# A gated cross-attention and mixture-of-experts block on one core: batches 2 and 3 prepared ahead of slot 0, the first values placed over two queues with the weight loads held behind them, K and V of chunk 2 in slot 0

## The reference

```python
def _L0_xattn_ref(x, y, Wq, bq, Wkv, bkv, Wo, bo):      # h = 16 heads, dh = 8
    q = (jnp.einsum('bld,ed->ble', x, Wq) + bq).reshape(b, l, h, dh)
    kv = (jnp.einsum('bmc,ec->bme', y, Wkv) + bkv).reshape(b, m, h, 2 * dh)
    k, v = (kv[..., :dh], kv[..., dh:])
    att = jax.nn.softmax(jnp.einsum('blhd,bmhd->blmh', q, k) * scale, axis=2)
    out = jnp.einsum('blmh,bmhd->blhd', att, v).reshape(b, l, d)
    return jnp.einsum('bld,ed->ble', out, Wo) + bo

def _more_forward(x, Wg, bg, W1, b1, W2, b2):           # E = 4 experts, top 2, R = 4 rounds
    cur = x
    for r in range(R):
        logits = flat @ Wg[r] + bg[r]
        ...                                             # softmax over the two best, weights cw
        hmid = jax.nn.gelu(jnp.einsum('nh,ehf->enf', flat, W1) + b1[:, None, :])
        y = jnp.einsum('enf,efh->enh', hmid, W2) + b2[:, None, :]
        cur = cur + jnp.einsum('ne,enh->nh', cw, y).reshape(b, s, h)
    return cur

x = x + jnp.tanh(g_xattn[0]) * _L0_xattn_ref(_layernorm(x), ctx_768, ...)
x = x + jnp.tanh(g_ffn[0]) * _L0_ffn_ref(_layernorm(x), ...)
```

## Time and profile before

| what | value |
|---|---|
| median of 3 runs | 466.93 us |
| the profiled execution | 467.07 us, of which the span of the engines is 465.3 us |
| PE busy | 451.0 us, 97% of the span |
| ACT, DVE, POOL busy | 370.3, 361.6, 69.6 us |
| attention stage | to 92.1 us, where the first expert matmuls start |
| fourth issue of SP, x of batches 2 and 3 | at 2.17 us |

### The profile page before, as it was taken

The page is one execution under the profiler, slowest core; times in us unless marked ns, Lnnn a source line. Parts: engine busy times, 40 slices in busy tenths (PEclk is TensorE's granted clock), DMA queues, the critical chain, the costliest instruction groups (busy, mean ns, idle before and its releaser), DMA issues.

```text
span 465.3 us, 8795 instructions
## 1 busy us (share of the span) xinstructions
PE 451.0 (97%) x2856; PEld 355.1 (76%) x2856; DVE 361.6 (78%) x723; ACT 370.3 (80%) x760; POOL 69.6 (15%) x107
## 2 busy tenths in 40 slices
PE   7599999999999999999999999999999999999996
PEld 6366767777877788878878887888788878888885
DVE  5569889988888779767876887688768876887776
ACT  5869998697878779877987798779877987787883
POOL 6968566125000000000000000000000000000000
PEclk9989999999999999999999999999999999999999
DMA  6870000050020200400040013002200310023001
GB/s 162 167 221 4 11 7 17 1 183 2 1 92 3 90 2 1 182 0 1 14 170 1 0 40 144 0 1 80 104 0 0 115 70 1 0 89 118 24 0 46
DMA packets 13085, 25.19 MB, mean 54 GB/s; under 512 B 4880, under 2 KB 8688, under 8 KB 10992
## 3 DMA queue, kind: packets, MB, share of 16 engines
q1 hardware_dynamic: 9792, 22.31, 13.9%
q0 software_dynamic: 2592, 2.10, 2.2%
q10 hardware_dynamic: 656, 0.23, 0.2%
HBM read 22.82 MB, written 1.18 MB: 52 GB/s over the span
## 4 chain that ended last, share of the span: by engine, by line
PE 94%; ACT 4%; issue 1%; DVE 0%; POOL 0%; POOLq 0%; ACTq 0%
PE ps L1390 13%; PE ps L1377 13%; PE ps L1392 13%; PE ps L1391 13%; PE ps L1379 13%; PE ps L1378 13%; PE ps L1259 4%; PE ps L1245 3%; ACT prob L702 3%; PE ps L1279 2%; PE ps L1285 2%; PE ps L1219 1%; PE ps L1344 1%; PE ps L1191 1%; PE ps L1292 1%
## 5 line engine op out<-in xcount | busy, mean ns | idle before, releaser
L941 DVE TENSOR_TENSOR h_lo<-g_sb,h_hi 128x512 fp32r<-128x512 f32 x256 | 170.0, 687 | 76.6 <-ACT h_hi L809 76.6
L802 ACT ACTIVATE g_sb<-ps,cols 128x512 f32<-128x512 f32 x256 | 174.5, 692 | 41.3 <-PE ps L1379 40.7
L809 ACT ACTIVATE h_hi<-g_sb 128x512 fp32r<-128x512 f32 x256 | 155.6, 639 | 0.0
L1390 PE MATMUL ps<-h_hi,w_hi 128*128 128x512 f32 x252 | 102.4, 406 | 0.0
L1377 PE MATMUL ps<-x_hi,w_hi 128*128 128x512 f32 x256 | 101.1, 395 | 0.0
L1379 PE MATMUL ps<-x_hi,w_lo 128*128 128x512 f32 x256 | 100.1, 391 | 0.0
L1378 PE MATMUL ps<-x_lo,w_hi 128*128 128x512 f32 x256 | 99.7, 390 | 0.0
L1392 PE MATMUL ps<-h_hi,w_lo 128*128 128x512 f32 x252 | 99.6, 395 | 0.0
L1391 PE MATMUL ps<-h_lo,w_hi 128*128 128x512 f32 x252 | 99.4, 395 | 0.0
L1390 PEld LDWEIGHTS ps<-h_hi,w_hi 128*128 128x128 f32 x252 | 47.3, 188 | 13.9 <-issue 2.7
L1379 PEld LDWEIGHTS ps<-x_hi,w_lo 128*128 128x128 f32 x256 | 48.0, 188 | 11.4
(11 more groups left out here) (125 smaller groups left out, 389.1 us busy)
## 6 DMA issues: line engine op xcount, KB each, us to landing
cwb_even<-cw_rows SPq DMA_DIRECT2D x8, 1024.0 KB, 5.4
cwb_odd<-cw_rows SPq DMA_DIRECT2D x8, 1024.0 KB, 4.8
w_hi<-in_L_ffn_W_dram POOLq DMA_DIRECT2D x2, 1024.0 KB, 10.0
w_in<-in_L_ffn_W_dram SPq DMA_DIRECT2D x1, 1024.0 KB, 8.7
x_sb<-in_x_dram SPq DMA_DIRECT2D x3, 256.0 KB, 5.3
out_dram<-xn SPq DMA_DIRECT2D x3, 256.0 KB, 2.5
ctxT<-in_ctx_dram SPq DMA_DIRECT2D x3, 115.5 KB, 5.0
v_st<-v_sb SPq DMA_DIRECT2D x16, 19.2 KB
```

The lines of the kernel that those rows point to most:

```text
L802: nc.scalar.activation(g_sb[:, k, :], ps[:, k, :], ACT.Gelu_apprx_tanh, bias=b1_c[:, e * NF + k:e * NF + k + 1]).then_inc(gelu_done, 1)
L809: nc.scalar.activation(h_hi[:, u % 2, k, :], g_sb[:, k, :], ACT.Copy).then_inc(hi_done, 1)
L941: nc.vector.tensor_tensor(h_lo[:, u % 2, k, :], g_sb[:, k, :], h_hi[:, u % 2, k, :].bitcast(F32), ALU.subtract).then_inc(lo_done, 1)
L1390: mm(yb, w2_hi[:, w], hh, start=k == 0, stop=False)
```

## The change

Batches 2 and 3 (part "c") are normalised, transposed and projected before slot 0. K of chunk 1 is copied by DVE. K and V of chunk 2 move into slot 0 and are copied by DVE. The 12 transfers of the first values are split, 8 on SP and 4 on POOL, and the four 1 MB weight loads wait until all 12 have landed. POOL's own prologue is put in another order, and several tables are moved by a slot. The warm matmuls go from 7 to 5.

```diff
@@ jobs and tables @@
-        job(("K", 1), "act", 4)
+        job(("XN", "c"), "act", 4)
+        job(("K", 1), "dve", 6)
         job(("V", 1), "act", 7)
+        job(("Q", "c"), "act", 5)
-        K_AT = {2: 2, 8: 3}
-        V_AT = {6: 2, 10: 3}
-        XN_AT = {0: "c", 2: 1, 3: 2, 8: 3}
-        Q_AT = {0: "c", 2: 1, 3: 2, 9: 3}
-        W_LAG = 0
+        K_AT = {8: 3}
+        V_AT = {10: 3}
+        XN_AT = {2: 1, 5: 2, 8: 3}
+        Q_AT = {2: 1, 5: 2, 9: 3}
+        W_LAG = 1
-        WD_AT = (1, 0)
+        WD_AT = (1, 1)
-        NORMALISE = {}
-        NORMALISE_P = {2: 1, 3: 2, 7: 3}
-        MOMENTS = {0: (0, 1), 1: (0, 2), 3: (0, 3), 8: (1, 0), 10: (1, 1), 15: (1, 2)}
+        NORMALISE = {1: 1}
+        NORMALISE_P = {4: 2, 7: 3}
+        MOMENTS = {0: (0, 1), 2: (0, 2), 4: (0, 3), 8: (1, 0), 10: (1, 1), 15: (1, 2)}
@@ SP @@
+        SP_PIECES = 8
             place_v(0)
+            sp.wait_ge(v_ld[0], 16 * SP_PIECES)
+            sp.wait_ge(v_side, 16 * (len(pieces) - SP_PIECES))
@@ POOL @@
-            nc.gpsimd.memset(v_st[:, 1, :, :, :, :], 0.0).then_inc(refill_done, 1)
+            row_heads_from()
             rstd_of(0, "a")
             rstd_of(0, "b")
+            rstd_of(0, "c")
             pool.wait_ge(headmask_ready, 1)
             stage_k(1)
-            rstd_of(0, "c")
-            row_heads()
-            expert_order()
-            pool.wait_ge(small_ld, 16)
-            pool.wait_ge(tg_ready, 1)
-            nc.gpsimd.tensor_scalar(bo_in[:, :], ...).then_inc(bo_gated, 1)
+            row_heads_to()
+            moved(pool, ("V", 0))
+            pool.wait_ge(fill_done, 1)
+            for z, j, k, row, row_end, m, m_end in pieces[SP_PIECES:]:
+                pool.dma_start(v_st[row:row_end, 0, k, z, DH * j:DH * (j + 1), :],
+                               v_sb[m:m_end, 0, z, DH * j:DH * (j + 1), :]).then_inc(v_side, 16)
+            nc.gpsimd.memset(v_st[:, 1, :, :, :, :], 0.0).then_inc(refill_done, 1)
             for b in range(B):
+                if b < 2:
+                    stage_k(b + 2)
+                if b == 0:
+                    ...                                  # the multiplication of bo_in
+                if b == 2:
+                    expert_order()
+                if b == 1:
+                    pool.wait_ge(v_ld[0], 16 * SP_PIECES)
+                    pool.wait_ge(v_side, 16 * (len(pieces) - SP_PIECES))
@@ DVE @@
             normalise("a")
+            moments(0, "c")
             stage_k0()
             normalise("b")
-            moments(0, "c")
+            normalise("c")
             ...
             shift(0)
-            normalise("c")
+            copy_k(1)
             written(dve, "BO")
             dve.wait_ge(bo_gated, 1)
             ...
+                if b in NORMALISE:
+                    normalise(NORMALISE[b])
+                if b == 0:
+                    copy_k(2)
+                    copy_v(2)
@@ PE @@
-            warm(bank("BO")[:, 0:P], 7)
+            warm(bank("BO")[:, 0:P], 5)
             project_q("b")
+            transpose_xn("c")
             project_k(1)
             project_v(1)
+            project_q("c")
             ...
+                if b == 0:
+                    project_k(2)
+                    project_v(2)
```

More of the change, by code:

```diff
@@ L196, in flamingo_gated_block @@
         refill_done = sem("refill_done")
+        v_side = sem("v_side")
         v_ld = [sem(f"v_ld{c}") for c in range(NC)]
@@ L324, in flamingo_gated_block @@
                 next_job(("V", V_AT[b]), "act")
+            if b == 0:
+                job(("K", 2), "dve", 6)
+                job(("V", 2), "dve", 7)
+                last_early.update({6: ("K", 2), 7: ("V", 2)})
         next_job(("CWT", 1), "cwT")
@@ L332, in flamingo_gated_block @@
         reads(("Q", "b"), "act")
-        reads(("K", 1), "act")
+        reads(("XN", "c"), "act")
+        reads(("Q", "c"), "act")
+        reads(("V", 1), "act")
+        reads(("K", 1), "dve")
         reads("BO", "dve")
+        reads(("K", 2), "dve")
+        reads(("V", 2), "dve")
         for b in range(B):
@@ L469, in place_v @@
                     sp.wait_ge(pv_done, TC * (c - 1))
-                for z, j, k, row, row_end, m, m_end in pieces:
+                for z, j, k, row, row_end, m, m_end in pieces[0:SP_PIECES] if c == 0 else pieces:
                     sp.dma_start(v_st[row:row_end, c % 2, k, z, DH * j:DH * (j + 1), :],
@@ L527, in _, with row_heads_from @@
                                     channel_multiplier=-1).then_inc(c_ready, 1)
-            def row_heads():
+            def row_heads_from():
                 nc.gpsimd.memset(row_head[:, :, :, :, :], 1.0).then_inc(row_step, 1)
@@ L537, in row_heads, with row_heads_to @@
                                             channel_multiplier=1).then_inc(row_step, 1)
+            def row_heads_to():
                 pool.wait_ge(row_step, 1 + NZ)
@@ L633, in _ @@
                     split_w(W_AT.index(b - W_LAG))
-                if b + 2 < B:
+                if 2 <= b < B - 2:
                     stage_k(b + 2)
@@ L759, in _ @@
             stage_q("b")
-            move_k(1)
+            move_xn("c")
             exponentials(0, 1)
@@ L763, in _ @@
             nc.scalar.activation(tgates[:, :], gates[:, :], ACT.Tanh).then_inc(tg_ready, 1)
+            stage_q("c")
             exponentials(0, 0)
+            move_v(1)
             for b in range(B):
@@ L872, in stage_k0, with copy_k, copy_v @@
                                         ALU.mult).then_inc(k_stage, 1)
+            def copy_k(c):
+                written(dve, ("K", c))
+                nc.vector.tensor_scalar(kT[:, TC * M * c:TC * M * (c + 1)], bank(("K", c))[:, 0:TC * M],
+                                        bk_c[:, 0:1], None, ALU.add).then_inc(job_dve, 1)
+            def copy_v(c):
+                written(dve, ("V", c))
+                nc.vector.tensor_copy(v_sb[:, c, :, :, :],
+                                      bank(("V", c))[0:M, :].rearrange("m (b z w) -> m z w b", z=NZ, w=HQ * DH)).then_inc(job_dve, 1)
             def smallest(b, half):
@@ L1094, in _ @@
             shift(0)
-            normalise("c")
+            dve.wait_ge(cols_ld, 16)
+            copy_k(1)
             written(dve, "BO")
@@ L1111, in _ @@
                     weights(0)
-                if b in NORMALISE:
-                    normalise(NORMALISE[b])
                 if b in PT_DVE:
@@ L1267, in weigh_values @@
                     moved(pe, ("PT", b, PT_DVE[b]))
-                pe.wait_ge(v_ld[c], 16 * len(pieces))
+                if c == 0:
+                    pe.wait_ge(v_ld[c], 16 * SP_PIECES)
+                    pe.wait_ge(v_side, 16 * (len(pieces) - SP_PIECES))
+                else:
+                    pe.wait_ge(v_ld[c], 16 * len(pieces))
                 if b == 0:
```

13 lines of the change are left out of this document (4 added, 9 removed).

## The result

The changed kernel takes 468.24 us (median of 8 runs, 467.9 to 469.03), beside 466.9 us for the kernel before (median of 8 runs, 466.14 to 467.49). The ratio is 1.0028, with an interval of 1.0019 to 1.0037. The time lies in the predicted range of 464.7 to 468.7, but the forecast was no change, 466.7, and the kernel is slower by more than its interval. The profiled execution took 469.03 us with a span of 467.2, against 467.07 and 465.3. It is the longest of the eight, and the only one whose mean granted clock was 0.996; the other seven have 0.999 or 1.000 and take 467.9 to 468.38.

What follows compares the result with a forecast made beforehand. PE was busy 97% of the span and the expert stage untouched, so only its earlier start could gain. Terms made -1.35 us at slot 7, +1.1 at slot 12: -0.25, forecast 466.7 us, 8-in-10 range 464.7 to 468.7.

Steps and rivals of the forecast that it cites:

- Slot 4 gains moments ... takes 4.6: Attention slot 4: with moments added on DVE, it takes 4.6 us against 4.11 before.
- Ahead of slot 0: Prologue: fewer warm matmuls, but DVE takes moments of batches 2 and 3 first; slot 0 at 12.0, +0.1 us.
- Slot 0, the wait for `bo_in`: DVE waits for POOL, whose four transfer issues take 3.4 us; slot 1 starts at 19.3 against 17.07, +2.2 us.
- Rival A: Faster, 465.0 us, chance 0.36: POOL issues take 0.68 (-0.65), and slots 12 to 14 make good the late `stage_k` (-1.1).
- Slot 1: Values land by 17.8, so the 2.72 us stall before `v_st` goes; slot 2 starts near 23.1 against 24.00.
- rival B: Slower, 468.4 us, chance 0.17: TensorE falls to half clock in slot 1 after PE's waits, +1.7 us.
- Slot 2: Q of chunk 1 ends last, behind DVE's work; slot 3 starts at 30.2 against 31.41, -1.2 us.
- Slots 3, 5 and 6: Attention slots: 4.15 us without projection and moments, 5.43 with transposes and Q of chunk 2, 4.15 without V.
- Slot 12: The weight piece in slot 11 delays POOL's `stage_k` of batch 13, so slot 12 starts late, +1.1 us.
- Weights: Weight loads start at 17.8 and end at some 31 us, first needed by DVE near 33.5; they fit by 2 us.
- C: Slower, 469.0 us, chance 0.09: POOL needs 1.42 us for each value transfer issue, +2.3 us.
- The lag: `W_LAG` = 1 runs slot 10's weight piece in slot 11 on POOL, ahead of `stage_k` of batch 13; +1.1 us.

Runs made afterwards that it cites:

- e10: Kernel e8 with DVE's moments of chunk 2 in slot 1 instead of slot 2; 463.28 us, ratio 0.9929 to the kernel before.
- e1: Changed kernel with POOL's `add_bias` of chunk 1 moved from slot 4's beginning to slot 5, behind `stage_k`; 467.26 us, ratio 1.0008.
- e2: Changed kernel with DVE's block holding the cast moved from slot 3 to slot 6, where POOL is busy without a gap; 473.41 us, ratio 1.0134.
- e4: Changed kernel with POOL's multiplication of `bo_in` right behind its four value transfers, ahead of the memset and `stage_k(2)`; 467.52 us, ratio 1.0018.
- e5: Changed kernel with seven warm matmuls instead of five; 468.73 us, ratio 1.0047.
- e6: Changed kernel with ACT's tanh earlier, POOL's `bo_in` multiplication ahead of its four value transfers, and `stage_k(2)` before the memset; 467.35 us, ratio 1.0011.
- e11: Changed kernel with DVE's moments of batches 2 and 3 behind `stage_k0` and the normalisation of batch 1; 468.5 us, ratio 1.0036.
- e3: Changed kernel with `W_LAG` back to 0 instead of 1; 466.53 us, ratio 1.0001.
- e8: Changed kernel with e1, e6, e5's seven warm matmuls, `stage_k(13)` first in slot 11, and chunk 1's moments ahead of the `bo_in` wait; 463.69 us, ratio 0.9939.
- e7: Kernel before with only the four 1 MB weight loads held until SP's 12 value transfers have landed; 465.72 us, ratio 0.9986.

## Why the prediction was wrong, step by step

**The step that failed: "Slot 4 gains moments ... takes 4.6".** It took 6.30, and 1.70 is most of the 2.16 us by which the sum was short (+1.91 measured, -0.25 predicted, both in the profiled execution). The moments did what they did in slot 8, where the shift started 3.80 after the slot: in e10, where the cast is short, it starts 3.81 after, and the slot takes 4.83, so 0.23 of the miss is the way from the shift's end to the next scores, priced too low. The rest, 1.47, is the cast of `wg_in` at the end of slot 3, which the sum had at nothing: after's shift started 5.27 after the slot. I had read DVE's and POOL's lines each for itself and asked only whether the weights would be there. They were; what stood in the way was POOL. Shown by five sizes of the one instruction: 0.17 with POOL idle (e10), 0.19 in before beside a `veps` of POOL of 0.25, 0.52 beside the end of one `k_st` (e1), 1.74 beside `k_st` and `add_bias` (after), 5.62 beside eight instructions (e2), and each of the last three ends 0.03 to 0.04 us after POOL's own end. In e4, e5, e6 and e11, which left both neighbours in place, it took 1.75 or 1.76. Before had missed the collision by luck: its `add_bias` ended at 35.77, its cast began at 35.84. The change took the moments out of slot 3, so DVE's cast came 3.39 us after the slot's start instead of 4.43, and it put POOL's normalisation of chunk 2 ahead of this `k_st`, which came at 3.17 instead of 2.42. So the two met.

The Trainium skill (SBUF — State Buffer, "Who interferes with whom") says that a cast or copy of VectorE may take a pair of ports that it shares with GpSimd, and that of the two the later one is blocked altogether, not slowed, for the whole of the other's instruction. This trace agrees with the block, with 1.74 us for 0.17 us of work, but not with its length: the cast was held over two instructions of POOL in after and over eight in e2. I had not held that rule against DVE's short instructions.

**What hid behind it.** The other steps missed by less, and partly against one another:

- *Ahead of slot 0*, +0.1 predicted, +0.75 measured. The normalisation of batches 2 and 3 took 1.02 beside POOL's `k_st` (8.46 to 9.16), against 0.59 in before, which looks like another collision of the same kind, though no run took it away; and the product for the bias row waited 0.32 for DVE's copy of K. By e11 the order of the moments was not the cause. The warm matmuls are not ruled out by e5.
- *Slot 0, the wait for `bo_in`*: right in kind, too large in size. POOL's four issues took 2.38 us, 0.60 each, below even my low end of 0.68, and not 3.4. `bo_row` came at 14.85 instead of 15.6, and slot 1 at 18.74 instead of 19.3. Rival A's first half was right, then, and more than right.
- *Slot 1*: the stall is gone, as predicted. That slot 2 would come 3.8 us after slot 1 was an error of mine, as the loop needs 4.1. And rival B's event came on top: half clock in 20 to 23 us, slot 1 at 5.04, where e1, e3 and e4 have 4.10 or 4.11 (their granted clock in 18 to 24 us was 1.00). That is 0.94 us, against the 1.7 at which I priced it. It belongs to the profiled execution: 469.03 less 0.94 is 468.1, an estimate that lies near the median of all eight. So the median's miss of 1.5 us, 468.24 against 466.7, holds the cast and not the clock.
- *Slot 2*: 6.94 measured, 7.1 predicted, ended by Q of chunk 1 as I had said (1.44, ACT's `q_st`). *Slots 3, 5 and 6*: 4.11, 5.43 and 4.10, all within 0.05.
- *Slot 12*: right. Slot 11 takes 5.31, +1.13 against +1.1, the wait is for `k_st` (1.28), and e3 takes both away. Rival A's second half, that slots 12 to 14 make it good, is wrong.
- *Weights*: nothing waited for the loads, though they ended later than the 31 us that I gave: in e3, POOL waited for `w_hi` until 33.80. C (+2.3 for slow issues) did not come.

**How the terms divide the time.** By medians, against after: the cast without `add_bias` is worth 1.0 us (e1), the bias row 0.9 (e6). The lag is worth 1.13 by the profile; e3's median, 1.7 less, holds the shorter cast of that run too. These three sum to 3.0, if they add, and e8, which has them with the moments ahead of the wait and seven warm matmuls, gains 4.5; how the other 1.5 divides was not run. So the change removed the stall that it was made to remove, and by this sum three small matters of order cost more than the 1.3 us by which it is slower than before. That the change without them beats before is not shown by e8 alone, as e8 also shortens a wait for `bo_in` that before has too (1.30 us in the earlier trace rows).

**What stays open.** Why the cast got in between two of POOL's instructions in e3 and not in e2 or after. Why the landing of x of batches 2 and 3 varies (3.2 to 4.4 us). With seven warm matmuls slot 0 moves with it (3.2: 11.65; 3.9: 12.33; 4.0: 12.40 and 12.42), with five it does not (3.8: 13.38; 4.3: 12.67). And why the clock falls in slot 1 in some executions and not in others: it fell after idle times of 1.82 (after), 1.83 (e11) and 1.86 us (e5), and did not after 1.77 (e2) and 1.60 (e3).

## What to carry to other kernels

When a change shifts one engine's work in time, lay the lines of VectorE and GpSimd side by side and look at what each short VectorE instruction on SBUF now runs beside: an instruction of 0.2 us can cost as much as its neighbour's whole run. Taking a wait away can show the next one right behind it, as in e4 and e7, so look for what stands there before you price the gain. Moving work ahead of a wait, as the moments in e8, is another way; what it gave alone was not run. Compare the granted clock of the other runs before you build on one profile: here the profiled execution of after had a half clock that seven of eight did not have. And before pricing a slot, check it against the loop's own least length.

## What the runs showed of the hardware

- A VectorE cast of 128x16 took 0.17 to 5.62 us, by what GpSimd ran beside it (e10, e2). The subtraction behind it, with both inputs in SBUF, took 0.17 alone (e1), and 0.65 and 0.70 beside GpSimd's `w_lo` (e3, e7).
- In after, GpSimd issued a small transfer from SBUF to SBUF in 0.60 us (four in 2.38), SyncE one in 0.78 (eight in 6.21). The two 1 MB loads took GpSimd 0.89 and 1.20 us to issue; in before they took 0.84 and 1.42.
- In e1's profile slot 0 came only at 14.59, as the matmuls ahead took about 1.8 times their usual length up to 14 us (V of chunk 1 1.91 instead of 1.04, the scores of batch 0 1.41 instead of 0.80), while the granted clock reads 1.00 there. 1.41 is also what the scores took at half clock in before (24.00 in the earlier trace rows). What held them the trace does not say.
